# Down product with stationary weights in f32r, made back two chunks later, and the rows of the means in f32r

## The reference, cut to what matters

```
for i in range(12):
    qkv = x @ Wqkv[i].T + bqkv[i]
    ...
    att = einsum(q, k) * scale          # 16 heads of 8, no softmax
    x = einsum(att, v) @ Wproj[i].T + bproj[i] + x
x = layernorm(x_in + x)
gate, up = x @ wg.T, x @ wu.T            # 384 hidden, weights integer / 127
x = layernorm(x + (silu(gate) * up) @ wd.T)
```

## Time and profile before

| | |
|---|---|
| median of three runs | 310.94 us (310.29 to 311.13) |
| the profiled execution | 309.86 us, its span 308.1 us |
| TensorE busy | 301.5 us (98%), granted clock 0.996 |
| VectorE busy | 226.6 us (74%) |
| ScalarE busy | 195.5 us (63%) |
| GpSimd busy | 123.6 us (40%) |
| token stage, first gate product to the end of the last down product | 250.2 to 302.5 us of the span |

### The profile page before, as it was taken

How to read it: one execution, slowest core, us unless ns; L and a number is a source line. 1 busy time by engine, 2 the same in 40 slices (tenths; PEclk the granted TensorE clock), 3 DMA queues, 4 the chain that set the end, 5 groups by cost and what they waited for, 6 DMA issues and landing times.

```text
span 308.1 us, 9537 instructions
## 1 busy us (share of the span) xinstructions
PE 301.5 (98%) x3951; PEld 281.2 (91%) x3951; DVE 226.6 (74%) x688; ACT 195.5 (63%) x481; POOL 123.6 (40%) x118
## 2 busy tenths in 40 slices
PE   8999999999999999999999999999999999999992
PEld 9989999899998998999989999899898889999982
DVE  0477587785876879758778587786975988888873
ACT  3449668587585775966749668587596275444550
POOL 3036252380543623525136152360445554556342
PEclk9999999999999999999999999999999999999998
DMA  7603020030120300303003010020000000211112
GB/s 269 262 2 115 4 79 36 4 113 2 22 95 3 116 0 5 113 2 110 8 2 115 3 51 30 4 80 2 2 2 2 2 2 2 66 38 35 36 34 72
DMA packets 8908, 14.96 MB, mean 49 GB/s; under 512 B 800, under 2 KB 5280, under 8 KB 8864
## 3 DMA queue, kind: packets, MB, share of 16 engines
q1 hardware_dynamic: 8144, 13.34, 13.2%
q10 hardware_dynamic: 720, 0.99, 0.9%
HBM read 12.23 MB, written 2.10 MB: 47 GB/s over the span
## 4 chain that ended last, share of the span: by engine, by line
PE 97%; DVE 1%; POOLq 0%; issue 0%; POOL 0%; ACT 0%
PE ps L964 14%; PE ps L1085 14%; PE ps L1033 8%; PE ps L1204 7%; PE ps L921 6%; PE ps L922 6%; PE ps L920 6%; PE ps L1001 5%; PE ps L983 4%; PE ps L1192 4%; PE ps L1193 4%; PE ps L1025 3%; PE ps L937 3%; PE ps L1164 2%; PE ps L990 2%; PE ps L975 2%
## 5 line engine op out<-in xcount | busy, mean ns | idle before, releaser
L448 POOL TENSOR_TENSOR step_lo<-step,step_hi 128x512 fp32r<-128x512 f32 (+1 forms) x44 | 52.1, 1219 | 41.0 <-ACT step_hi L556 41.0
L419 POOL TENSOR_TENSOR wq_lo<-w,wq_hi 128x512 fp32r<-128x512 f32 x12 | 15.4, 1280 | 100.6 <-ACT wq_hi L533 100.6
L920 PE MATMUL ps<-state_hi,step_hi 128*128 128x258 f32 x165 | 47.5, 288 | 0.0
L921 PE MATMUL ps<-state_lo,step_hi 128*128 128x258 f32 x165 | 46.6, 283 | 0.0
L922 PE MATMUL ps<-state_hi,step_lo 128*128 128x258 f32 x165 | 46.6, 283 | 0.0
L964 PE MATMUL ps<-w,gram 128*128 128x128 f32 x352 | 42.8, 275 | 0.0
L964 PEld LDWEIGHTS ps<-w,gram 128*128 128x128 f32 x352 | 41.9, 192 | 0.6
L529 ACT COPY gk<-ps 128x512 f32<-128x512 f32 x48 | 28.1, 586 | 20.6 <-PE ps L964 20.6
L1085 PE MATMUL ps<-step,gram 128*128 128x128 f32 x320 | 38.7, 279 | 0.0
L1085 PEld LDWEIGHTS ps<-step,gram 128*128 128x128 f32 x320 | 36.8, 191 | 0.8
L576 ACT COPY gram<-ps 128x256 f32<-128x256 f32 x88 | 32.8, 373 | 4.7
(11 more groups left out here) (140 smaller groups left out, 639.4 us busy)
## 6 DMA issues: line engine op xcount, KB each, us to landing
w<-weights SPq DMA_DIRECT2D x12, 592.5 KB, 3.8
xchan<-x_chan SPq DMA_DIRECT2D x8, 256.0 KB, 4.2
out<-xchan SPq DMA_DIRECT2D x7, 256.0 KB, 2.3
xt<-x_tok SPq DMA_DIRECT2D x4, 258.0 KB, 5.6
xt<-x_tok ACTq DMA_DIRECT2D x3, 258.0 KB, 5.3
fw_int<-ffn_weights SPq DMA_DIRECT2D x1, 576.0 KB, 5.7
cst<-consts SPq DMA_DIRECT2D x1, 147.5 KB, 7.2
xt<-x_tok SPq DMA_DIRECT2D x1, 129.0 KB, 2.6
```

Source lines behind the costliest of these rows:

```text
L448: nc.gpsimd.tensor_tensor(split_group(step_lo, g), split_group(step, g), split_group(step_hi_f, g), ALU.subtract).then_inc(step_lo_ready, 1)
L920: nc.tensor.matmul(dst, l_hi, r_hi, start=True, stop=False)
L921: nc.tensor.matmul(dst, l_hi, r_lo, start=False, stop=False)
```

## The change

Four things change.

1. **Down product.** The down weights are kept as integers and split like the gate and up weights (`wgu_hi` grows to three parts; scale moved into `SCALE_HID`). For chunks 0 to 6 `down_t_stage(n)` has the weights stationary and streams 512 tokens: three f32r passes with `hid_hi` and three with `hid_lo`, result channel-major. `down_copy` (ScalarE) takes it out of PSUM, and `down_back_stage` multiplies each 128 tokens of it by `project` (identity minus 1/128), which transposes it and takes its mean off. `hid_hi` is a cast on ScalarE, three times a chunk; `hid_lo` is a subtraction on POOL for j = 0 and 1 and on VectorE for j = 2. The last chunk keeps the float32 form, in banks 0 and 1.
2. **Order.** Down of chunk c-1 is done in chunk c of TensorE; y and var2 of chunk c-2 in chunk c of VectorE; var1(c+1) moves from the end of VectorE's chunk c-1 to the start of its chunk c; norm2(c-2) is in POOL's chunk c. `h1` gets four buffers.
3. **x not centred.** `centre`, `xc`, `mu0` and `neg_mu0` are gone; z reads `xchan` itself, and the constant part uses the difference of the means instead.
4. **Rows of the means in f32r.** From layer 1 on, `rows_stage` is three f32r passes of 256 columns and stands behind all four pairs of groups 0 and 1 instead of behind three. VectorE splits the means ahead of each layer (two instructions of 128x128), POOL splits the key and value weights (two of 128x256). `LOW_LAYER` moves from 5 to 6, and its reduction covers 1152 columns.

```diff
@@ gpsimd, layer
+                if not first:
+                    pool.wait_ge(w_in[s], at(8, 16 - 8 * s))
+                    pool.wait_ge(mean_done, at(1, 0))
+                    nc.gpsimd.tensor_copy(wkv_hi[:, :], w[:, s, WK:WK + 2 * P]).then_inc(wkv_hi_ready, 1)
+                    pool.wait_ge(wkv_hi_ready, at(1, 0))
+                    nc.gpsimd.tensor_tensor(wkv_lo[:, :], w[:, s, WK:WK + 2 * P], wkv_hi[:, :].bitcast(F32),
+                                            ALU.subtract).then_inc(wkv_lo_ready, 1)
@@ gpsimd, chunks
-                if ahead >= 2:
-                    pool.wait_ge(h1_ready, (c + 1) * CT + CT)
-                    rstd1_part(c + 2)
-                if ahead > 0:
-                    norm2(c)
-                if ahead >= 4:
-                    pool.wait_ge(z_done, c + 3)
-                    centre(c + 4, slot)
+                if 1 <= c < CHUNKS - 1:
+                    pool.wait_ge(h1_ready, c * CT + CT)
+                    rstd1_part(c + 1)
+                if c >= 1:
+                    hid_low(c - 1, 1)
+                if c >= 2:
+                    norm2(c - 2)
+                if c < CHUNKS - 1:
+                    hid_low(c, 0)
...
+            norm2(CHUNKS - 2)
@@ scalar, chunks
+            def hid_high(n, j):
+                act.wait_ge(hid_ready, n * HC + (HC + j + 1))
+                if n >= 2:
+                    act.wait_ge(down_t_done, n - 1)
+                nc.scalar.copy(hid_hi[:, n % 2, j, :], hid[:, j, :]).then_inc(hid_hi_ready, 1)
+
+            def down_copy(n):
+                act.wait_ge(down_t_done, n + 1)
+                if n:
+                    act.wait_ge(down_done, n)
+                nc.scalar.copy(down_t, ps[:, DOWN_BANK, :]).then_inc(down_t_ready, 1)
...
                 gate(c, 0)
-                if c == 0:
-
-                    gate(c, 1)
+                gate(c, 1)
                 if not last:
-                    norm1(c + 1, 1 - slot)
-                if c:
-                    gate(c, 1)
+                    norm1(c + 1)
                 gate(c, 2)
                 if not last:
                     ht_copy(c + 1)
+                    hid_high(c, 0)
+                if c:
+                    down_copy(c - 1)
+                if not last:
+                    hid_high(c, 1)
+                    hid_high(c, 2)
@@ vector, layer
+                if not first:
+                    dve.wait_ge(mu_ready, at(PAIRS, PAIRS))
+                    nc.vector.tensor_copy(means_hi[:, :], means[:, :]).then_inc(means_hi_ready, 1)
+                    dve.wait_ge(means_hi_ready, at(1, 0))
+                    nc.vector.tensor_tensor(means_lo[:, :], means[:, :], means_hi[:, :].bitcast(F32),
+                                            ALU.subtract).then_inc(means_lo_ready, 1)
@@ vector, chunks
+                if n and j < HC - 1:
+                    dve.wait_ge(hid_lo_first_ready, (HC - 1) * (n - 1) + j + 1)
...
-                for j in range(HC):
-                    hid_part(c, j)
-                if ahead >= 1:
+                if 1 <= c < CHUNKS - 1:
+                    dve.wait_ge(rstd1_ready, c + 1)
+                    var1_part(c + 1, (c + 1) % 2)
+                if c >= 2:
+                    y_part(c - 2)
+                hid_part(c, 0)
+                hid_part(c, 1)
+                if c >= 2:
+                    var2_part(c - 2)
+                hid_part(c, 2)
+                if c < CHUNKS - 1:
                     ht_part(c + 1)
-                if ahead >= 2:
-                    z_part(c + 2, c + 2, slot)
-                    dve.wait_ge(rstd1_ready, c + 2)
-                    var1_part(c + 2, slot)
-                if ahead == 0:
-                    return
-                y_part(c, slot)
-                var_part(c, y, y_ready, 2, sq2, var2, var2_ready)
+                    hid_low_last(c)
+                if c < CHUNKS - 2:
+                    z_part(c + 2, c + 2, c % 2)
@@ tensor, rows and chunks
+                    pe.wait_ge(means_hi_ready, at(1, 0))
+                    pe.wait_ge(wkv_lo_ready, at(1, 0))
+                    nc.tensor.matmul(rows_out, means_hi[:, :], wkv_hi[:, :], start=True, stop=False)
+                    nc.tensor.matmul(rows_out, means_hi[:, :], wkv_lo[:, :], start=False, stop=False)
+                    pe.wait_ge(means_lo_ready, at(1, 0))
+                    nc.tensor.matmul(rows_out, means_lo[:, :], wkv_hi[:, :], start=False, stop=True).then_inc(mean_done, 1)
...
+                if c == 0:
+                    pe.wait_ge(z_ready, 2)
+                    z_stage(2)
+                    ht_stage(1)
+                    return
+                if c + 1 < CHUNKS:
+                    ht_stage(c + 1)
+                down_t_stage(c - 1, low)
+                if c + 2 < CHUNKS:
                     pe.wait_ge(z_ready, c + 2)
-                    z_stage(c + 2, c + 2, slot)
-                if z_first:
-                    ht_stage(c + 1, 1 - slot)
-                down_stage(c, last_chunk=ahead == 0)
+                    z_stage(c + 2)
+                down_back_stage(c - 1)
+                if c == CHUNKS - 1:
+                    last_down_stage()
```

More of the change, by code:

```diff
@@ L626, in _ @@
                     .then_inc(nu_part_own_ready, 1)
-            norm1(0, 0)
+            norm1(0)
             ht_copy(0)
@@ L631, in _ @@
             for c in range(CHUNKS):
-                chunk(c, c % 2, last=c == CHUNKS - 1)
+                chunk(c)
             t = CT - 1
@@ L895, in _ @@
             for c in range(CHUNKS):
-                chunk(c, c % 2, CHUNKS - 1 - c)
-            last_slot, parts = 1, [range(CT)[part] for part in halves]
+                chunk(c)
+            y_part(CHUNKS - 2)
+            var2_part(CHUNKS - 2)
+            last_slot, parts = (CHUNKS - 1) % H1_BUFS, [range(CT)[part] for part in halves]
             for h in range(2):
@@ L1194, in gate_stage, with down_t_stage, of, down_back_stage @@
                             .then_inc(done, 1)
-            def down_stage(n, last_chunk=False):
+            def down_t_stage(n, low):
+                out = ps[:, DOWN_BANK, :]
                 pe.wait_ge(y_ready, n + 1)
+                def of(part, j):
+                    return part[:, 2 * HIDDEN + P * j:2 * HIDDEN + P * (j + 1)]
+                for j in range(HC):
+                    pe.wait_ge(hid_hi_ready, n * HC + (j + 1))
+                    nc.tensor.matmul(out, of(wgu_hi, j), hid_hi[:, n % 2, j, :], start=j == 0, stop=False)
+                    if low:
+                        nc.tensor.matmul(out, of(wgu_lo, j), hid_hi[:, n % 2, j, :], start=False, stop=False)
+                for j in range(HC):
+                    if j < HC - 1:
+                        pe.wait_ge(hid_lo_first_ready, (HC - 1) * n + j + 1)
+                    else:
+                        pe.wait_ge(hid_lo_last_ready, n + 1)
+                    last = nc.tensor.matmul(out, of(wgu_hi, j), hid_lo[:, n % 2, j, :], start=False, stop=j == HC - 1)
+                last.then_inc(down_t_done, 1)
+            def down_back_stage(n):
+                pe.wait_ge(down_t_ready, n + 1)
+                for t in range(CT):
+                    last = nc.tensor.matmul(ps[:, DOWN_BANK, P * t:P * (t + 1)], down_t[:, P * t:P * (t + 1)], project,
+                                            start=True, stop=True)
+                last.then_inc(down_done, 1)
+            def last_down_stage():
+                n = CHUNKS - 1
                 def products_of(j, tokens, first=(), final=()):
@@ L1244, in _, with chunk @@
             pe.wait_ge(nub_ready, 2)
-            def chunk(c, slot, low, ahead=2):
+            def chunk(c, low):
                 pe.wait_ge(ht_lo_ready, c + 1)
@@ L1263, in chunks @@
                     pe.wait_ge(a_ready, GROUPS)
-                    with loop(pe, CHUNKS // 2 - 1) as i:
-                        for s in range(2):
-                            chunk(i * 2 + s, s, low)
-                for c in range(CHUNKS - 2 if low else 0, CHUNKS):
-                    chunk(c, c % 2, low, CHUNKS - 1 - c)
+                for c in range(CHUNKS):
+                    chunk(c, low)
             with nc.If(low_part[0] == 0):
```

193 lines of the change are left out of this document (101 added, 92 removed).

## The result

| | before | after |
|---|---|---|
| median of the runs | 310.94 us (310.29 to 311.71) | 329.64 us (328.33 to 330.13) |
| the profiled execution | 309.86 us, span 308.1 us | 328.33 us, span 326.5 us |
| TensorE busy | 301.5 us (98%) | 306.5 us (94%) |
| ratio after / before | | 1.0605, 95% interval 1.0582 to 1.0628 |

What follows compares the result with a forecast made beforehand. TensorE, 98% busy, bounded the kernel before; afterwards a dependency ring through all engines would. Token stage +15.2, rows -0.8, layer 6 +0.3 make +14.7: 324.6 us profiled, 325.6 as median with 1.08 added; range 319 to 332.

Steps and rivals of the forecast that it cites:

- the ring: Token stage: each norm1 depends on the previous chunk's norm1 through every engine's in-order queue; 8.07 us, 8.2 with contention.
- dear contention: Token-stage rival: POOL's SBUF sharing stretches VectorE, 8.7 us and more a chunk, 328.6 us; chance 0.10 within range, 0.04 beyond.
- those for "right": Whole kernel: chain spread over all engines, gates 8.2 us apart, TensorE idle ahead of transpositions, layers of 19.8 us.
- signs for "wrong": Token stage: TensorE above 95% busy, granted clock under 0.95, or z(c+2) out of PSUM before hid_lo(c,2) is done.
- Part 1: TensorE's own work: 0.39 us less in each of seven chunks (-2.7), rows of the means -0.8, layer 6 +0.26.
- Part 2: Token stage, middle chunks: the ring sets a period of 8.2 us against TensorE's 6.41, idling it some 1.7 a chunk.
- the first link: Start of the ring: four scaled copies on ScalarE, then TensorE's ht ending 0.16 after them; 1.44 us.
- The contention: VectorE's instructions beside POOL's subtractions in the token stage: 0.1 us a chunk, upper bound 0.6.
- Parts 3 and 4: First chunks and end of the token stage: norm1(2) at 260.1 us; serial end of 3.96 us, costing 3.2.
- The short ring: Token-stage rival: hand-overs overlap and casts are faster, about 7.5 us a chunk, 321 us; chance 0.07 for below 319.
- That TensorE alone counts: Token-stage rival: TensorE finds every operand ready, so the change gives -3.2 us, 307.7 us; chance 0.04.

Runs made afterwards that it cites:

- no_pool_low: The kernel after without POOL's two subtractions a chunk (low parts of hidden blocks 0 and 1 left out): 325.17 us, ratio 1.0470.
- three_mends: The kernel after with z(c+2) ahead of hid_low_last, zero products in TensorE's wait, own buffers for the last chunk's y, variance and rstd: 323.73 us.
- low_after_z: The kernel after with z(c+2) taken out of PSUM ahead of hid_low_last(c) in VectorE's queue: 325.06 us, ratio 1.0468.
- swap_no_pool: The kernel after with z(c+2) ahead of hid_low_last(c) and without POOL's two subtractions a chunk: 318.55 us, ratio 1.0243.

## Why the prediction was right, and which terms were off

The time lies in the range, and the direction and the ring are right. But 329.6 is outside the 321 to 329 that the forecast gave to its own sum. It lies in the part that was given to dear contention, with 0.10. Some luck is in it: the end of the span was 1.2 us shorter than before, for which the forecast had nothing, and hid a quarter of the surplus of the turns.

Of the signs named, those for "right" are there: the chain is spread, ScalarE's largest wait is norm1 for rstd (10.6 us), TensorE's is ahead of the transpositions (8.6 us, put down to the copies), a layer lasts 19.82, one 19.97, and z comes after hid_low_last. The gates are 8.2 to 8.8 apart, and 10.4 twice. Of the two signs for "wrong" one is there too: the granted clock was 0.94 over the token stage, under the 0.95 that was named.

**Part 1** holds. Three passes of 0.12 stand for one product of 0.43, and down_t and its way back cost 1.4 and 0.94 for a forecast of 1.40 and 0.89. (A float32 product of 256 columns thus costs as much as three and a half f32r passes of that width, not two; the two that the trace lists for it are long ones. The forecast took both from rows.) A layer lasts 19.82 for 19.89, and the longer one 0.15 more where 0.26 was expected. The first gates start 0.62 us earlier for a forecast of 0.5, but that start differs by up to 1.9 us between the edits of the kernel after, whose layers are the same. With gates 2.80, ht 0.57 and z 0.89 a chunk of TensorE's own work is 6.58, for a forecast of 6.41 and for 6.80 before. The saving exists, smaller than forecast, and no turn of any run is short enough to let it count.

**Part 2** has a ring that is there with every link, and two terms too small. Its base was 8.07; no_pool_low measures 8.31. Nearly all of that is the first link, 1.44 in the forecast and 1.66 in the chain: it added 0.16 behind the last scaled copy from the timeline, but the end of a transposition was read in the chain, where matmuls are listed some 0.2 later. The contention was put at 0.1 a chunk with an upper bound of 0.6; it is 0.45 in the turns that have it. The row that the forecast had the earlier trace rows was read as a price of 0.1 for each sum. Its ends say otherwise: the sum ended at 250.71, 0.15 after `centre` (250.56), just as all the later ones do. The first ring's stretch is therefore not a price of its own instructions but the time for which POOL's still run, and that is set by the second ring, which part 2 did not lay out. Without it the forecast's ring would have given 8.3 a turn. That the upper bound of 0.6 came near is chance. Four turns of 0.45 are 1.8 us (the fourth with its pause), five of 0.11 (8.31 less 8.2) another 0.5.

**Parts 3 and 4** hold to 0.3 us: norm1(2) at 259.63 for 259.6, the serial end 3.97 for 3.96. The forecast of the end lists POOL's sequence of subtraction, hid, var2, rstd2 and norm2 one by one. That is half of the second ring. What it failed to do was to ask whether this sequence closes in the middle chunks too; it does, at 8.75.

**The rivals.** The short ring (319 or less) needs both rings cut, and work left out, to come to 318.6. Dear contention forecast 328.6 by 0.5 a chunk and comes nearest, with the clock on top. That TensorE alone counts is refuted by the turns, 8.75 for its 6.58 of work.

**What stays open.** Why the clock fell in these two stretches and not in the turns between. Whether a second buffer of `hid` would open the second ring was not tried; by the base ring of 8.31 it could not have brought the kernel below the one before. A queue order in which neither hid_low_last nor the casts lie between down_t and var1 was not tried either.

## What to carry to other kernels

Before a consumer is moved one or two chunks later, write out one period as a ring through every in-order queue, and then look for a second ring: each engine's own sequence, followed until it comes back to itself through a buffer that is used again. Where two rings share an instruction that waits inside itself, the shorter one looks as full as the longer, an edit that shortens it shows nothing, and only both cuts together tell what they cost. The ends of such instructions, set beside those of the other engine, tell which waits for which. A busy share below 100% on every engine is no slack in such a schedule: the 0.2 us a chunk saved on the engine that bounded the kernel were paid with 2.2 us of waiting, and the part that kept its place in the queue (the rows of the means) was the only one that gave anything.

## What the runs showed of the hardware

- A VectorE instruction with two inputs in SBUF that started 0.09 us or more behind a POOL instruction on 128x512 tiles never ended before it in these traces. A sum of squares of 128x128 (0.28 us alone), where it was held up, ended 0.14 to 0.16 after POOL's subtraction whether it took 0.56 or 1.38, and so it did after `centre` in the kernel before (0.38) and after norm2's multiplication by a broadcast in three_mends (1.09). A subtraction of 128x512 (0.69 alone) ended 0.54 to 0.56 after POOL's, at lengths up to 1.58. A sum of squares has the same tile as both its inputs. POOL's subtraction, begun while VectorE's ran, took 1.74 for 1.26 and ended 1.15 after it. Beside POOL's rstd (128x4) the sums kept their 0.29.
- In the kernel after, the wait of TensorE ahead of ht was 1.90, 1.09, 1.53, 1.51 and 1.60 us in the five turns. Passes of down_t of 0.42 for 0.233 followed the longest, 1.90, and slow passes the next longest, 1.60, and none of the others. But in low_after_z slow passes followed waits of 1.52, twice, so the length of the last wait alone doesn't decide. In swap_no_pool it was 0.92 once and then 0.24, and the clock stayed at 1.00.
- low_after_z had two chunks of 10.3 and 10.2 us at a clock of 0.83 while its turns stayed at 8.75 to 8.90: where the ring that binds doesn't pass TensorE, slow passes only fill its waiting, and holding the clock brought 0.3 to 0.7 us (ratios, medians) instead of 2.8 to 3.1.
